# Two 64-row slots a pass on the two column halves of the array, in the last expert stage of a graph network kernel

## The reference, cut to what matters

```python
logits = x @ gate_w + gate_b                     # x: 625 x 512, 8 experts
topk_vals, topk_idx = top_k(logits, 2)
gates = softmax(topk_vals)
for each node and each of its 2 experts e:
    h = relu(x @ w1[e] + b1[e])                  # 512 -> 1024
    y += gate * (h @ w2[e] + b2[e])              # 1024 -> 512
```

## Time and profile before

| | us |
|---|---|
| median of 3 runs | 2436.04 (2435.09 to 2436.72) |
| the profiled execution | 2432.22 |
| its span | 2430.5 |
| routed loop of the last layer, first row transposes to the end | 267.3 |

### The profile page before, as it was taken

How to read it: one execution, slowest core, us unless ns; L and a number is a source line. 1 busy time by engine, 2 the same in 40 slices (tenths; PEclk the granted TensorE clock), 3 DMA queues, 4 the chain that set the end, 5 groups by cost and what they waited for, 6 DMA issues and landing times. The chain is left out here.

```text
span 2430.5 us, 39014 instructions
## 1 busy us (share of the span) xinstructions
PE 2278.4 (94%) x14326; PEld 1510.7 (62%) x14326; DVE 1113.9 (46%) x2631; ACT 703.1 (29%) x1366; POOL 614.5 (25%) x624
## 2 busy tenths in 40 slices
PE   5798969999999999999999999999999997989998
PEld 4475537766766765647657567566665665567775
DVE  8732895545545556545425325326262333530102
ACT  0423343322333332315315315325211211112111
POOL 0463666505524530010100100101113442111110
PEclk9898989999999999999999999999989998989999
DMA  3122017516525542011011011010026766458885
GB/s 92 43 69 85 1 55 226 150 35 219 149 60 177 168 128 103 13 47 53 23 45 53 24 45 53 23 54 34 22 114 222 253 210 204 116 220 318 311 293 197
DMA packets 68400, 285.96 MB, mean 118 GB/s; under 512 B 18650, under 2 KB 18778, under 8 KB 60286
## 3 DMA queue, kind: packets, MB, share of 16 engines
q1 hardware_dynamic: 35771, 192.15, 22.8%
q0 software_dynamic: 32448, 91.31, 12.4%
HBM read 407.54 MB, written 26.23 MB: 178 GB/s over the span
## 5 line engine op out<-in xcount | busy, mean ns | idle before, releaser
L86 PE MATMUL ps<-XT,W 128*128 128x250 f32 (+1 forms) x1200 | 334.8, 435 | 3.5 <-ACT XT L1420 1.6
L86 PEld LDWEIGHTS ps<-XT,W 128*128 128x128 f32 x1200 | 228.9, 193 | 106.5 <-issue 22.2
L1150 PE MATMUL ps<-XN,W 128*128 128x512 f32 x498 | 258.9, 603 | 2.6 <-ACT GT L1472 2.6
L1856 POOL TENSOR_TENSOR H<-H,RB 125x512 f32<-125x512 f32 x40 | 50.5, 1267 | 724.3 <-DVE XN L2179 611.7
L86 PE MATMUL ps<-W,HT 128*128 128x512 f32 (+1 forms) x312 | 141.5, 608 | 0.8 <-ACT HT L3242 0.5
L86 PEld LDWEIGHTS ps<-HT,W 128*128 128x128 f32 x1088 | 126.9, 195 | 8.7 <-issue 7.7
L86 PE MATMUL ps<-HT,W 128*128 128x128 f32 x1088 | 127.1, 279 | 0.8 <-DVE HT L3253 0.8
L2572 POOL DMA_INDIRECT result_rows<-KT,LOGC x61 | 62.1, 1018 | 251.2 <-DVE KT L3273 197.2
L1126 POOL DMA_INDIRECT XT<-node_rows,LOGC x81 | 77.2, 953 | 174.4 <-DMA node_rows<-V 122.3
L1288 PEld LDWEIGHTS ps<-P,QT 128*128 128x128 f32 x672 | 89.9, 195 | 45.0 <-issue 45.0
L1288 PEld LDWEIGHTS ps<-P,KT 128*128 128x128 f32 x672 | 88.1, 192 | 39.7 <-issue 39.7
(11 more groups left out here) (666 smaller groups left out, 4593.6 us busy)
## 6 DMA issues: line engine op xcount, KB each, us to landing
W<-in_L_ffn_Wgud SPq DMA_DIRECT2D x92, 960.0 KB
W<-in_L_ffn_w SPq DMA_DIRECT2D x36, 2048.0 KB, 8.4
W<-in_L_gnn_Wqkv SPq DMA_DIRECT2D x4, 3072.0 KB, 9.9
H<-in_L_ffn_Wgud SPq DMA_DIRECT2D x11, 960.0 KB
XN<-in_L_ffn_Wgud SPq DMA_DIRECT2D x11, 960.0 KB
V<-in_L_ffn_Wgud SPq DMA_DIRECT2D x11, 960.0 KB
P<-in_L_ffn_Wgud SPq DMA_DIRECT2D x11, 960.0 KB
RB<-in_L_ffn_Wgud SPq DMA_DIRECT2D x11, 960.0 KB
```

Source lines behind the costliest of these rows:

```text
L86: last = nc.tensor.matmul(out, lhs(k), rhs(k), start=(k == 0), stop=(k == nk - 1))
L1150: nc.tensor.matmul(b.ps[:, n % PR, :], b.EAT[:, t * 128:(t + 1) * 128], We[layer], start=True, stop=True)\
L1856: ins = nc.gpsimd.tensor_tensor(b.H[0:R, t, :], b.H[0:R, t, :], b.RB[0:R, at:at + D], ALU.add)
```

## The change

A slot is 64 rows, and two slots make a pass: 14 passes (`NU`) of an even and an odd slot, the even one on the array's columns 0 to 63 and partitions 0 to 63 of the result, the odd one on columns 64 to 127. The rows of a pass are still 128, gathered and transposed together.

- First layer: the 64 rows are the stationary operand and 512 columns of `w1` the moving one, for a low and a high half of the 1024 hidden columns (banks `LOW` and `HIGH`). The result has rows on partitions, so each half is copied out (`hid`, ScalarE for low, VectorE for high), transposed in 4 pieces in the full array (`hidden_turned`), and only then gets its bias (VectorE, `biased`) and relu (ScalarE). The second layer has the pieces of 64 rows as the stationary operand.
- Bias: all of `b1` is loaded once and each pass picks its two experts' columns with `owner_hot` (`bias_picked`).
- Weights: the odd slot's weights have a ring of 3 homes in `b.W` and 3 in the new `b.ROOM`, which takes the place of the tensors XN, H, V, XT, CNT and P. The even slot reads its own home (index 3) only if its expert is neither that of the odd slot in the same pass nor of the odd slot in the pass before; otherwise it reads their home, by an address in a register (`read_home`). Loads carry a condition and move nothing where it is 0.
- `l3_block` computes the owners, conditions and homes for that, on VectorE, and waits for `expert` to reach 3 before the first load. Its table matmuls are done for even and odd slots apart.
- The rows at the end are read back into `b.W`, and SyncE waits for the last pass's first layers (`hid_mm`) before it starts.

```diff
 class WideExpertSlots(Route):
-    GR, early = 4, 2
+    GR, RING, HOME = 4, 3, 4096
...
+    def read_step(self, sp, u):
+        regs = self.step_registers[u % 4]
+        sp.load(regs, self.steps[0:1, 4 * u:4 * u + 4])
+        return [sp.snap(x, min_val=0, max_val=self.ne - 1 if i < 2 else 1) for i, x in enumerate(regs)]
+
+    def read_home(self, pe, u):
+        return pe.value_load(self.home_of[0:1, u:u + 1], min_val=0, max_val=self.RING * self.HOME)
+
+    def load(self, sp, name, homes, step, half, home, done):
+        at = self.HOME * home
+        sp.dma_start(homes[:, at:at + self.HOME], self.weights(name, step[half]), cond=step[2 + half])\
+            .then_inc(done[home], 16)
...
 def l3_block
-            sp.wait_ge(s["expert"], 1)
-            for sl in range(r3.early):
-                r3.load_first(sp, sl)
-                r3.load_second(sp, sl)
+            sp.wait_ge(s["expert"], 3)
+            step = r3.read_step(sp, 0)
+            r3.load_first(sp, step, 1, 0)
+            r3.load_first(sp, step, 0, RING)
             sp.wait_ge(p.f3_stored, 32 * (T + K))
+            r3.load_second(sp, step, 1, 0)
+            r3.load_second(sp, step, 0, RING)
...
-                nc.tensor.matmul(b.ps[:, 1, 0:NS + 1], place_hot[j], tables[j], start=(j == 0), stop=(j == T * K - 1))\
-                    .then_inc(s["table_mm"], 1)
+                for h in range(2):
+                    last = nc.tensor.matmul(b.ps[64 * h:64 * h + 64, 1, 0:NU + 1], place_hot[j],
+                                            tables[j][:, (NU + 1) * h:(NU + 1) * (h + 1)], start=(j == 0),
+                                            stop=(j == T * K - 1), tile_position=(0, 64 * h))
...
+            c.mark(v.tensor_scalar(to_own, home_before, -1.0, float(RING * r3.HOME), ALU.mult, ALU.add))
+            c.mark(v.tensor_tensor(to_before, home_before, home_now, ALU.subtract))
+            c.mark(v.memset(from_before, 1.0))
             dve.wait_ge(s["slots"], 1)
             dve.wait_ge(s["base_mm"], 1)
...
+            c.link(v.tensor_copy(owner, b.ps[:, 5, 128:128 + NS]))
+            c.mark(v.tensor_scalar(clipped, owner[0:1], float(NE - 1), None, ALU.min))
+            c.mark(v.tensor_tensor(from_odd, even_of, odd_of, ALU.not_equal))
+            c.mark(v.tensor_tensor(from_before[:, 1:NU], even_of[:, 1:NU], odd_of[:, 0:NU - 1], ALU.not_equal))
+            c.mark(v.tensor_scalar(odd_has, odd_of, float(NE), None, ALU.is_lt))
+            c.mark(v.tensor_tensor(odd_new[:, RING:NU], odd_of[:, RING:NU], odd_of[:, 0:NU - RING], ALU.not_equal))
+            c.wait()
+            v.tensor_copy(steps[:, :, 0:2], clipped.rearrange("p (u h) -> p u h", h=2)).then_inc(s["expert"], 1)
+            c.mark(v.tensor_tensor(even_new, from_odd, from_before, ALU.mult))
+            c.mark(v.tensor_tensor(odd_new[:, RING:NU], odd_new[:, RING:NU], odd_has[:, RING:NU], ALU.mult))
+            c.mark(v.tensor_copy(odd_new[:, 0:RING], odd_has[:, 0:RING]))
+            c.mark(v.tensor_tensor(move, to_own, from_before, ALU.mult))
+            c.wait()
+            v.tensor_copy(steps[:, :, 2], even_new).then_inc(s["expert"], 1)
+            v.tensor_copy(steps[:, :, 3], odd_new).then_inc(s["expert"], 1)
+            c.link(v.tensor_tensor(move, move, to_before, ALU.add))
+            c.link(v.tensor_tensor(move, move, from_odd, ALU.mult))
+            c.link(v.tensor_tensor(home, home_now, move, ALU.add))
+            v.tensor_copy(r3.home_of, home).then_inc(s["expert"], 1)
...
 def l3_routed_block
+            steps = [r.read_step(sp, u) for u in range(RING)]
+            for u in range(1, RING):
+                r.load_first(sp, steps[u], 1, u)
+                r.load_second(sp, steps[u], 1, u)
+            for u in range(1, NU):
+                later = u + 1 if RING <= u + 1 < NU else None
+                if later:
+                    steps.append(r.read_step(sp, later))
+                sp.wait_ge(s["hid_mm"], 2 * u)
+                r.load_first(sp, steps[u], 0, RING)
+                if later:
+                    r.load_first(sp, steps[later], 1, later % RING)
+                sp.wait_ge(s["y_mm"], u)
+                r.load_second(sp, steps[u], 0, RING)
+                if later:
+                    r.load_second(sp, steps[later], 1, later % RING)
+            sp.wait_ge(s["hid_mm"], 2 * NU)
...
+            def first(u, bank, at, ks):
+                odd = r.HOME * (u % RING)
+                for k in ks:
+                    col = 2 * HALF * k + at
+                    nc.tensor.matmul(b.ps[EVEN, bank, :], xT[u % 2][:, k, EVEN], b.W[:, col:][:, bass.ds(even, HALF)],
+                                     start=(k == 0), stop=(k == KD - 1), tile_position=(0, 0))
+                    last = nc.tensor.matmul(b.ps[ODD, bank, :], xT[u % 2][:, k, ODD], b.W[:, odd + col:odd + col + HALF],
+                                            start=(k == 0), stop=(k == KD - 1), tile_position=(0, 64))
...
+                first(u, LOW, 0, range(KD)).then_inc(s["hid_mm"], 1)
...
+                first(u, HIGH, HALF, (0, 1))
+                pe.wait_ge(s["low_raw"], u + 1)
...
+                hidden_turned(LOW_T, 0)
+                first(u, HIGH, HALF, (2, 3)).then_inc(s["hid_mm"], 1)
+                if u + 1 < NU:
+                    rows_transposed(u + 1)
...
+                pe.wait_ge(s["ready"], 2 * u + 1)
...
+                second(u, (0,))
+                pe.wait_ge(s["high_raw"], u + 1)
...
+                hidden_turned(HIGH_T, 1)
+                second(u, (1,))
+                if u + 1 < NU:
+                    following = r.read_home(pe, u + 1)
+                second(u, (2, 3))
+                pe.wait_ge(s["ready"], 2 * u + 2)
+                second(u, (4, 5, 6, 7)).then_inc(s["y_mm"], 1)
```

More of the change, by code:

```diff
@@ L2625, in load_first @@
[L2625 to L2633, removed]
+        lf = b.LOGC[:, :, :].rearrange("p t n -> p (t n)")
@@ new lines, in read_home, with load_first, load_second @@
+    def read_home(self, pe, u):
[4 more added lines that the diff above has]
+            .then_inc(done[home], 16)
+    def load_first(self, sp, step, half, home):
+        self.load(sp, "L3_ffn_w1", self.b.W, step, half, home, self.w1_in)
+    def load_second(self, sp, step, half, home):
+        self.load(sp, "L3_ffn_w2", self.b.ROOM, step, half, home, self.w2_in)
@@ new lines, in hidden_turned, with second @@
+            def hidden_turned(bank, half):
+                for m in range(4):
+                    last = nc.tensor.transpose(b.ps[:, bank, 128 * m:128 * (m + 1)], hid[half][:, 128 * m:128 * (m + 1)],
+                                               b.ident[:, :])
+                last.then_inc(s["turned"], 1)
+            def second(u, ms):
+                odd = r.HOME * (u % RING)
+                for m in ms:
+                    nc.tensor.matmul(b.ps[EVEN, 6 + u % 2, :], hT[u % 2][:, 128 * m:128 * m + 64],
+                                     b.ROOM[:, D * m:][:, bass.ds(even, D)],
+                                     start=(m == 0), stop=(m == H2 - 1), tile_position=(0, 0))
+                    last = nc.tensor.matmul(b.ps[ODD, 6 + u % 2, :], hT[u % 2][:, 128 * m + 64:128 * (m + 1)],
+                                            b.ROOM[:, odd + D * m:odd + D * (m + 1)],
+                                            start=(m == 0), stop=(m == H2 - 1), tile_position=(0, 64))
+                return last
@@ new lines, in _ @@
+            rows_out(0)
+            bias_picked(0)
+            for u in range(NU):
+                if u:
+                    result_out(u - 1)
+                dve.wait_ge(s["turned"], 2 * u + 1)
+                dve.wait_ge(s["bias"], 2 * u + 2)
+                if u >= 2:
+                    dve.wait_ge(s["y_mm"], u - 1)
+                biased(u, LOW_T, 0)
+                dve.wait_ge(s["hid_mm"], 2 * u + 2)
+                if u:
+                    dve.wait_ge(s["turned"], 2 * u)
+                v.tensor_scalar(hid[1], b.ps[:, HIGH, :], 1.0, None, ALU.mult).then_inc(s["high_raw"], 1)
+                if u + 1 < NU:
+                    rows_out(u + 1)
+                dve.wait_ge(s["turned"], 2 * u + 2)
+                biased(u, HIGH_T, 1)
+                if u + 1 < NU:
+                    bias_picked(u + 1)
@@ L3474 @@
     routes = []
[L3475 removed]
+    for i, (ne, k, ns, size) in enumerate(((64, 6, 45, 32), (8, 2, 14, 64))):
         assert ns * 128 // size >= (k * N + ne * (size - 1)) // size
```

273 lines of the change are left out of this document (158 added, 115 removed).

## The result

The changed kernel takes 2411.17 us (median of 4 runs, 2406.93 to 2414.15), the kernel before 2435.62 us beside it: ratio 0.9897 with a 95% interval of 0.9885 to 0.9908, 24.5 us less. A second comparison gave 2413.15 against 2434.65 us, 0.991 (0.9894 to 0.9926). Forecast were 2414.0 us, 2404 to 2428. The profiled execution has a span of 2412.2 us.

A forecast was written before the change was run, and what follows sets the result against it. TensorE was taken to bound the last stage: 1.43 to the first matmul, 3.1 low clock, 13 x 15.9 passes, 7.7, 22.85 and 3 at the end, +0.5 ahead, 245.3 for 267.3 us; 2414.0 us, range 2404 to 2428.

The forecast's parts named there:

- TensorE sets the stage, so time is passes times pass: Last stage, from about 2163 us: bound by TensorE and nothing else, so its price is slots times time per slot.
- Full overlap of the halves, 0.429 us a round: Matmul pairs in a pass: both halves run at the same time, 13.74 us a pass; 27.5 us if not.
- The quarters: Narrow-expert stage before the change: four 32-column quarters overlapped without loss, 0.268 us a round, taken as evidence for two halves.
- Rival (c): Matmul pairs: halves overlap only in part; with no overlap +192 us, 2606 us; chance 0.06.
- factor of 2.38 for three column tiles: Skill document's measured gain instead of 3; at 1.26 times the pair time, pass 19.5 us and kernel 2463 us.
- Register address free: 16 register-addressed matmuls a pass: no cost while work is queued, 0.74 us a pass at worst.
- Three groups of transposes, 2.1 us a pass: In each pass, three groups of 4 transposes interrupt the half-array matmuls: 2.1 us with mode switches, bounds 1.3 to 3.3.
- Weights no bound: Weight loads in the passes: 48 MB instead of 68, a 2 MB load lands in 8.4 us, no wait.
- List longer by some 1.5 us, gather 1 us shorter, +0.5 together: Ahead of the stage: about 2.0 us more VectorE work, table matmuls 0.5 less, gather 1 less; sum +0.5 (-3 to +3).
- First pass at 1.2 GHz, 3.1 us: Start of the stage: first matmuls run at 1.2 GHz after TensorE idles, and the 3.1 us this costs stay.
- Read-back 3.6 us later, and it sets the end: End: rows land in `b.W`, so SyncE waits for the last first layers; read-back starts 3.6 us later, setting the end.
- Clock in the last ten records, +3 us: Final placing matmuls: TensorE idles 5.8 us, clock falls to 1.2 GHz, +3 us (0 to 4.3).

The follow-up runs named there:

- full-array kernel: Changed kernel with both slots of a pass multiplied in one full-array matmul using the even slot's weights, never tiled; pass 15.05 us, ratio 0.9857.
- in turn: Changed kernel with all even matmuls of a group given before its odd ones; 2437.48 us, pass 17.83 us.
- fixed address: Changed kernel with the even half reading the odd half's home at a fixed address, without register operations; pass 15.95 us, ratio 0.9909.
- second later: Changed kernel with the first pass's second-layer weights (2 MB) loaded at the start of the routed loop, not in the routing block; ratio 0.9895.
- free home: Changed kernel with the final rows read back into home 2 of W and ROOM, without waiting for the last pass's first layers; ratio 0.9892.

## Why the prediction was right, point by point

- **TensorE sets the stage, so time is passes times pass.** Right. 14 passes for 17 slots, no hole in either, and taking two passes away gave 31.9 us.
- **Full overlap of the halves, 0.429 us a round.** Right: halves 0.01 us apart, and the full-array kernel shows that a pair costs no more than one matmul. The quarters were good evidence for it. The prediction said nothing of how it comes about, and the picture that I had of it later was wrong: order in the program matters little (17.83 us in turn). Rival (c) at no overlap was not built as such: where the overlap was forbidden in one direction the pass rose by 10.5 us, against 13.7 for both. The factor of 2.38 for three column tiles that I had taken from "TensorE: Matmul & The Clock Gate", Part 3, in the Trainium skill as a sign against the change doesn't show here.
- **Register address free.** Right, shown by the fixed address. The working from the earlier trace rows was loose: 125 columns at the rate of 512 are 0.105 us and not 0.109, so it allowed 0.05 us in 4 matmuls and not 0.02.
- **Three groups of transposes, 2.1 us a pass.** 2.22 us measured: 12 x 0.107 and 3 x 0.30 to 0.31. I had 0.28 from the earlier trace rows. My upper bound of 3.3 us doesn't follow from its own terms: 12 x 0.107 and six switches of 0.27 are 2.9; neither bound was needed. "TensorEngine Tiling (Array Packing)", Key Properties, in the Trainium skill states a drain at each change of mode. The trace agrees with a loss of 0.30 us for leaving and entering, 0.15 us a switch if both cost the same.
- **Pass 15.9 us.** 15.947 us.
- **Copies covered.** Right: in the windows TensorE is never idle.
- **Weights no bound.** Right, with 12 loads; DMA share 0.75 to 0.80 in the full passes.
- **List longer by some 1.5 us, gather 1 us shorter, +0.5 together.** The list grew by 0.83 us: the VectorE part between the owners' matmul and the gates grew by 1.8 us (0.30 before, 2147.52 to 2147.82, 2.08 from 2152.04 to 2154.12), and the table matmuls gave 1.05 back (3.24 for 4.29), twice what I had. The gather was mis-signed: 8.43 and 8.79 us, 0.3 to 0.7 more. I had taken the 8 MB before as the measure of what delays it; 4 MB ahead are as bad, and only fewer than that (second later) helped: 3.7 us from giving to landing for 8.4. Sum +1.2 for +0.5.
- **First pass at 1.2 GHz, 3.1 us.** The clock was back to 2.4 GHz 3.2 us after the first matmul, for 5.9 before, so it cost some 1.7 us. In four of the experiments, where TensorE idled 1.80 to 2.69 us before the row transposes, it didn't fall there at all.
- **Read-back 3.6 us later, and it sets the end.** Right: free home gave 4.0 us back.
- **Clock in the last ten records, +3 us.** The clock fell, but was back before they ended: 6.59 us for 4.53, +2.1. TensorE idled 6.76 us before them, not 5.8.
- **Sum.** From the first row transposes to the end 244.8 forecast, 243.3 and 243.2 measured. The errors are +0.7 for the passes, -1.4 for the clock in the first pass and -0.9 for the tail there, and +0.7 for list and gather ahead. That they leave only 0.8 us (-22.0 forecast, -22.8 in the trace) is luck.

The forecast rested on four terms (rounds, groups, tail, list) that the experiments moved one by one, so it was right for its own reasons, but the closeness of the number isn't earned: the gather's sign was wrong, and the price of the low clock was set too high in both places.

## What to carry to other kernels

When a stage is bound by TensorE, count records and mode switches: two column halves cost what one full matmul costs here (0.43 us a round of 512 fp32 columns), and each excursion from the tiled mode 0.3 us, so put transposes together. Packing pays where it saves passes, 14 for 17 here, not by making a pass faster. Packing buys fewer rounds only if the overlap is there, and the way to see it is in the start times of the two halves. A buffer that is freed by the last matmuls can set the end of a kernel: give late transfers a home that nothing near the end reads. Weigh edits of a few us by stretches between fixed instructions, since totals of this kernel vary by more than that.

## What I had not expected of the hardware

- With even and odd matmuls given in groups, one half starts ahead of up to four records of the other that stand before it. Groups of two matmuls a half lose nothing. Groups of four put one half four records behind, and the pass pays for that once, 1.7 of its 1.9 us, where transposes make both halves finish.
- TensorE idled 3.32 us before and kept 2.4 GHz, idled 3.07 us in the kernel with the free home and was at 1.2 GHz for part of the next 6.2 us. Whether an idle time of some 3 us costs the clock can't be told from its length in these runs; 2.6 us of needless matmuls in that gap kept 2.4 GHz.
- A gather of 128 rows took 3.6 to 3.7 us from giving to landing with no weights or 2 MB of them given before it, and 8.1 to 8.7 us with 4 or 8 MB, in the two kernels and the experiments named above.
- Two executions of the same code reach the routing up to several us apart (2144.60 and 2148.17 for the changed kernel). What makes that difference was not looked into.
